# An LSTM-like recurrence: one of four state operations a step goes from VectorE to GpSimd

## The chip, the core and the metric

The kernel runs on one core of a Trainium2 chip, as one program. The metric is the device time of one execution in microseconds (us); the median of several runs counts. A core has five engines with a queue each: TensorE (PE in the profile; its weight loads are PEld), VectorE (DVE), ScalarE (ACT), GpSimd (POOL) and SyncE (SP). They work in parallel and wait for each other by semaphores.

## What is computed

The reference takes 3125 rows of 256 features and 50000 edges through four graph layers, each followed by a feed-forward part. The second of these parts is a recurrence over the 3125 rows, and it alone is touched by the change:

```python
def step(carry, xs):
    h, c = carry
    xi_t, xf_t, xg_t, xo_t = xs
    i_t = jax.nn.sigmoid(xi_t + h @ V_i)
    f_t = jax.nn.sigmoid(xf_t + h @ V_f)
    g_t = jnp.tanh(xg_t + h @ V_c)
    o_t = jax.nn.sigmoid(xo_t + h @ V_o)
    c_new = h * c + i_t * g_t
    h_new = o_t * jnp.tanh(c_new)
    return ((h_new, c_new), h_new)
(_, _), hs = lax.scan(step, (h0, c0), (xi, xf, xg, xo))
```

The new state c is h * c + i * g; the gate f has no effect on the output.

## The kernel before

The stages run one after the other, with a barrier of the engines between them. The recurrence is the stage of `Sweeps.run`. It doesn't go through the 3125 rows one by one: they are cut into 125 chains of 25 rows (`NC` and `L`), all chains take a step at once, and `FREE` = 9 sweeps over the 25 rows pass each chain's last state on to the next chain as its start. That makes 225 steps, written out one by one. At the end the largest change of the last sweep is computed (L2057 to L2070); with the inputs here it lets the kernel go on without further sweeps.

A state has 256 values. They lie as two halves (x = 0 and 1) of 128 partitions each, with the 125 chains along the columns. So h, c and each of the three gates used is 2 x 128 x 125 float32, and a step has six gate rows (`g` = 0 to 5): the candidate and the input gate of half 0, the same of half 1, and the output gate of halves 0 and 1. What each engine does in a step `n`, in the order of its queue:

- **TensorE** (L1970): for each `g` two products of a 128x128 weight block with half `y` of the old h. In float32 each product is two matmul instructions in the trace, so there are 24. First come the three products `g` = 0, 1, 2 with half 0 of h, then the same with half 1, and then the rest. The step begins when half 0 of the new h is there; half 1 is first needed by its seventh matmul instruction. `then_inc(gated, 1)` reports a finished `g`.
- **ScalarE**: sets the inputs of the output gates into PSUM (L2011), the gates `g` = 0 to 3 (L2001) into `Gt`, tanh of half 0 of c into `t3` (L2006, `state(n, 0)`), the output gates `g` = 4 and 5 (L2001), tanh of half 1 of c (`state(n, 1)`). Each raises `acted` by 1.
- **VectorE**: puts the inputs of coming gates into PSUM (L2024), `t1` = old h * old c for both halves (L2046); then for x = 0 and x = 1 `t2` = `Gt[x]` * `Gt[4 + x]` (L2028) and new c = `t1` + `t2` (L2030); then half 0 of the new h (L2034, `output(n, 0)`), inputs (L2024), half 1 of the new h (L2034), inputs. Each raises `stepped`, ten times in a step.
- **GpSimd** and SyncE have no instruction in these steps.

An engine runs its queue in the order written, so an instruction that waits holds all behind it. `t1`, `t2`, `t3`, `Gt` and `Cs` (c within a sweep) exist once and are reused in each step.

Of the kernel before, what the change touches and what calls it, by code (L numbers as in the profile page):

```python
# [16 lines left out]
ALU = mybir.AluOpType  # L17
# [1885 lines left out]
class Sweeps:  # L1903
# [33 lines left out]
    def run(self, sweeps, again):  # L1937


        k, nc = self.k, self.k.nc  # L1940
        gated, acted, stepped = k.loop
        XG, HS, V, Gt, t1, t2, t3, df, ft = (self.XG, self.HS, self.V, self.Gt, self.t1, self.t2, self.t3, self.df,
                                             self.ft)
        first, steps = 0, sweeps * L

        def sums(n, g, count=1):
            at = g + 6 * (n % 2) if g < 2 else g
            return k.PS[:, at:at + count, 0:NC]

        with k.block() as block:  # L1950
            @block.tensor
            def _(e):
                for b in range(8):
                    e.matmul(k.PS[:, b, 0:NC], V[:, 0, 0, :], k.ident[:, 0:NC], start=True, stop=True)

            if again:
                @block.vector
                def _(e):
                    e.tensor_copy(self.H[0][:, :, :], self.H[1][:, :, :])
                    e.tensor_copy(self.C[0][:, :, :], self.C[1][:, :, :])  # L1960
            else:
                @block.gpsimd
                def _(e):
                    for b in self.H + self.C:
                        e.memset(b[:, :, :], 0.0)
        with k.block() as block:
            @block.tensor
            def _(e):
                def product(n, g, y):
                    return e.matmul(sums(n, g)[:, 0, :], V[:, y, (4, 0, 5, 1, 2, 3)[g], :], self.old_h(n)[:, y, :],  # L1970
                                    start=False, stop=y == 1, skip_group_check=True)

                for n in range(first, first + steps):
                    r = n - first
                    e.wait_ge(stepped, 10 * r - 1 if r > 0 else 2)
                    product(n, 0, 0)
                    product(n, 1, 0)
                    if r > 0:
                        e.wait_ge(stepped, 10 * r)
                    product(n, 2, 0)  # L1980
                    if r > 0:
                        e.wait_ge(stepped, 10 * r + 1)
                    product(n, 0, 1).then_inc(gated, 1)
                    product(n, 1, 1).then_inc(gated, 1)
                    product(n, 2, 1).then_inc(gated, 1)
                    if r > 0:
                        e.wait_ge(stepped, 10 * r + 2)
                    product(n, 3, 0)
                    product(n, 3, 1).then_inc(gated, 1)
                    e.wait_ge(acted, 9 * r + 1)  # L1990
                    for g in (4, 5):
                        product(n, g, 0)
                        product(n, g, 1).then_inc(gated, 1)
                e.wait_ge(stepped, 10 * steps + 7)
                e.transpose(k.PS[0:1, 7, 0:128], df[:, 2:3], k.ident[:, :]).then_inc(gated, 1)

            @block.scalar
            def _(e):
                def gate(n, g, row):
                    e.wait_ge(gated, 6 * (n - first) + g + 1)  # L2000
                    e.activation(Gt[:, row, :], sums(n, g)[:, 0, :],  # L2001
                                 ACT.Tanh if row >= 4 else ACT.Sigmoid).then_inc(acted, 1)

                def state(n, x):
                    e.wait_ge(stepped, 10 * (n - first) + 6 + 2 * x)
                    e.activation(t3[:, x, :], self.new_c(n)[:, x, :], ACT.Tanh).then_inc(acted, 1)  # L2006

                for n in range(first, first + steps):
                    if n > first:
                        e.wait_ge(acted, 9 * (n - first) - 1)  # L2010
                    e.activation(sums(n, 4, 2), XG[:, n % L, 4:6, :], ACT.Copy).then_inc(acted, 1)  # L2011
                    gate(n, 0, 4)
                    gate(n, 1, 0)
                    gate(n, 2, 5)
                    gate(n, 3, 1)
                    state(n, 0)
                    gate(n, 4, 2)
                    gate(n, 5, 3)
                    state(n, 1)

            @block.vector
            def _(e):
                def inputs(n, g, row, count=1):
                    e.tensor_copy(sums(n, g, count), XG[:, n % L, row:row + count, :]).then_inc(stepped, 1)  # L2024

                def state(n, x):
                    e.wait_ge(acted, 9 * (n - first) + 3 + 2 * x)
                    e.tensor_tensor(t2[:, x, :], Gt[:, x, :], Gt[:, 4 + x, :], ALU.mult).then_inc(stepped, 1)  # L2028
                    e.wait_ge(stepped, 10 * (n - first) + 5 + 2 * x)
                    e.tensor_tensor(self.new_c(n)[:, x, :], t1[:, x, :], t2[:, x, :], ALU.add).then_inc(stepped, 1)  # L2030

                def output(n, x):
                    e.wait_ge(acted, 9 * (n - first) + 7 + 2 * x)
                    e.tensor_tensor(self.new_h(n)[:, x, :], Gt[:, 2 + x, :], t3[:, x, :],  # L2034
                                    ALU.mult).then_inc(stepped, 1)

                inputs(first, 0, 0, 2)
                inputs(first, 2, 2, 2)
                for n in range(first, first + steps):
                    r = n - first  # L2040
                    if r > 0:
                        e.wait_ge(acted, 9 * r - 6)
                    inputs(n + 1, 0, 0, 2)
                    if r > 0:
                        e.wait_ge(stepped, 10 * r + 1)
                    e.tensor_tensor(t1[:, :, :], self.old_h(n), self.old_c(n), ALU.mult).then_inc(stepped, 1)  # L2046
                    state(n, 0)
                    state(n, 1)
                    output(n, 0)
                    inputs(n + 1, 2, 2)  # L2050
                    output(n, 1)
                    inputs(n + 1, 3, 3)
                h = [b[:, :, 1:NC] for b in (self.H[(sweeps + 1) % 2], self.H[sweeps % 2])]
                c = [b[:, :, 1:NC] for b in (self.C[(sweeps + 1) % 2], self.C[sweeps % 2])]
                nb = NC - 1
                e.wait_ge(stepped, 10 * steps + 1)
                e.tensor_tensor(t1[:, :, 0:nb], h[1], h[0], ALU.subtract).then_inc(stepped, 1)  # L2057
                e.tensor_tensor(t2[:, :, 0:nb], c[1], c[0], ALU.subtract).then_inc(stepped, 1)
                e.tensor_copy(HS[:, L - 1, :, :], self.new_h(first + steps - 1))
                e.wait_ge(stepped, 10 * steps + 4)  # L2060
                e.tensor_reduce(df[:, 0:1], t1[:, :, 0:nb], AX.XY, ALU.max,
                                apply_absolute_value=True).then_inc(stepped, 1)
                e.tensor_reduce(df[:, 1:2], t2[:, :, 0:nb], AX.XY, ALU.max,
                                apply_absolute_value=True).then_inc(stepped, 1)
                e.wait_ge(stepped, 10 * steps + 6)
                e.tensor_tensor(df[:, 2:3], df[:, 0:1], df[:, 1:2], ALU.max).then_inc(stepped, 1)
                e.wait_ge(gated, 6 * steps + 1)
                e.tensor_reduce(ft[:, 0:1], k.PS[0:1, 7, 0:128], AX.X, ALU.max).then_inc(stepped, 1)
                e.wait_ge(stepped, 10 * steps + 8)
                e.tensor_scalar(self.go_on[:, :], ft[:, 0:1], TOL, None, ALU.is_gt)  # L2070
        nc.multi_engine_barrier(list(mybir.ALL_ENGINES), sems_to_clear=range(gated.num, stepped.num + 1))


def gate_inputs(k, XG, V):
# [981 lines left out]
def program(nc, a):  # L3056
    k = Core(nc, a)
    with ExitStack() as top:
# [6 lines left out]
        k.XR = nc.dram_tensor("rows_x", (N, D), f32).ap()  # L3065
        k.YT = nc.dram_tensor("rows_y", (2 * N + P + SLOTS * 128, D), f32).ap()
        k.EP = nc.dram_tensor("table", (ROWE, W * 4), f32).ap()
        k.loop = [nc.alloc_semaphore(s) for s in ("gated", "acted", "stepped")]
        k.slow = [nc.alloc_semaphore(s) for s in ("slow_step", "slow_landed0", "slow_landed1", "slow_landed2")]
        k.early = Sig(nc.alloc_semaphore("counts_early"))  # L3070
        k.first_out = [Sig(nc.alloc_semaphore(s)) for s in ("first_neg_out", "first_adj_out")]
# [95 lines left out]
```

## Time and profile before

| what | us |
|---|---|
| median of 3 runs (4396.59 to 4404.05) | 4402.93 |
| the profiled execution | 4404.55 |
| its span, first to last instruction | 4402.2 |
| the 225 steps of the recurrence, 2085 to 2821 | 736 |
| one step, from one start of TensorE to the next | 3.26 |

The profile is one execution. Its page gives busy times over the whole span, in which the stages have different limits; a question about the recurrence is answered by views that are cut to its stretch. Within it the steps repeat with almost equal times, so the rows of one step stand for all.

### The profile page before, as it was taken

To read this page: it belongs to the slowest core of one execution; us is meant where nothing else is said; L and a number is where in the kernel's file an instruction comes from. 1 tells how busy PE (TensorE), PEld (TensorE's weight loads), DVE (VectorE), ACT (ScalarE), POOL (GpSimd) and SP (SyncE) were. 2 spreads that over 40 slices of the span, in tenths; PEclk is the share of its full clock that TensorE was granted. 3 is DMA by queue.
4 is the path that set the end of the run, shared out by engine and by line. 5 is a ranking of instruction groups with operands and counts; after the bars stand their busy time and mean duration, and the time that the engine had idled before them with its cause. 6 is when DMAs were issued, how large, how long until landed. Compare 5 with 4: busy or idle time off the path is not lost. (4 is left out here: it accounts for less than half of the span.)

```text
span 4402.2 us, 67329 instructions
## 1 busy us (share of the span) xinstructions
PE 3539.8 (80%) x23858; PEld 3112.2 (71%) x23858; DVE 2759.3 (63%) x7024; ACT 1645.3 (37%) x4317; POOL 1261.6 (29%) x1266
## 2 busy tenths in 40 slices
PE   4677874755777876998999999799999699959696
PEld 3565653643565665784888888689999699949695
DVE  6899996563888848873888888732234433353444
ACT  1344442212444444562666666521110223320131
POOL 6777751635777710000000000000000122200263
PEclk8788786977887887999999999999998799979798
DMA  5455543244555563500000000143444311153424
GB/s 157 133 159 144 158 117 106 89 109 120 145 159 143 158 157 111 139 12 15 1 1 1 1 1 1 39 116 108 122 117 159 106 38 38 34 136 108 138 72 130
DMA packets 196536, 418.06 MB, mean 95 GB/s; under 512 B 54821, under 2 KB 127659, under 8 KB 195840
## 3 DMA queue, kind: packets, MB, share of 16 engines
q1 hardware_dynamic: 135296, 250.07, 19.8%
q0 software_dynamic: 60928, 164.04, 13.1%
q8 instruction: 171, 2.80, 0.3%
q14 instruction: 141, 1.16, 0.1%
HBM read 329.61 MB, written 84.35 MB: 94 GB/s over the span
## 5 line engine op out<-in xcount | busy, mean ns | idle before, releaser
L825 POOL DMA_INDIRECT sb<-features,sb x850 | 836.3, 984 | 262.1 <-issue 258.5
L1970 PE MATMUL ps<-sb 128*128 128x125 f32 x5400 | 662.1, 279 | 74.0 <-DVE sb L2034 72.9
L1970 PEld LDWEIGHTS ps<-sb 128*128 128x128 f32 x5400 | 619.8, 192 | 116.3 <-DVE sb L2034 115.0
L2269 PE MATMUL ps<-sb 125*125 125x256 f16 x5000 | 571.9, 275 | 15.8 <-DVE sb L2369 15.8
L2269 PEld LDWEIGHTS ps<-sb 125*125 125x125 f16 x5000 | 559.4, 138 | 21.0 <-issue 16.0
L136 POOL IOTA sb<- 128x56 f32 (+9 forms) x30 | 5.5, 219 | 1645.7 <-POOLq L105 1562.1
L2001 ACT ACTIVATE sb<-ps 128x125 f32<-128x125 f32 x1350 | 344.4, 273 | 232.5 <-PE ps L1970 202.7
L2982 ACT ACTIVATE sb<-ps,sb 128x128 f32<-128x128 f32 x784 | 221.1, 376 | 551.3 <-PE ps L2910 551.3
L1122 PE MATMUL ps<-sb 128*125 128x260 f32 x1700 | 385.7, 386 | 11.3 <-PEq L1120 10.8
L2910 PE MATMUL ps<-sb 128*128 128x128 f32 x3136 | 385.6, 279 | 1.9 <-DVE sb L2951 1.9
L1122 PEld LDWEIGHTS ps<-sb 128*125 128x125 f32 x1700 | 317.9, 189 | 93.6 <-issue 42.3
L2910 PEld LDWEIGHTS ps<-sb 128*128 128x128 f32 x3136 | 371.5, 195 | 2.6 <-DVE sb L2951 2.5
L2924 PE MATMUL ps<-sb 128*128 x1568 | 366.3, 380 | 0.0
L2924 PEld LDWEIGHTS ps<-sb 128*128 128x128 f32 x1568 | 285.6, 191 | 32.3 <-issue 0.3
L613 PE MATMUL ps<-sb 128*125 128x392 bf16 x850 | 247.2, 473 | 69.1 <-PEq L611 67.5
L2887 POOL DMA_INDIRECT rows_y<-sb x168 | 193.0, 1149 | 380.0 <-DVE sb L2963 365.0
L1343 PE MATMUL ps<-sb 125*125 125x257 f32 x1250 | 280.1, 386 | 17.2 <-DVE sb L1441 10.8
L1343 PEld LDWEIGHTS ps<-sb 125*125 125x125 f32 x1250 | 237.2, 191 | 58.2 <-issue 16.7
L613 PEld LDWEIGHTS ps<-sb 128*125 128x125 bf16 x850 | 166.4, 204 | 137.3 <-issue 76.1
L2944 DVE COPY sb<-sb 128x512 f32 (+2 forms) x168 | 133.9, 797 | 182.3 <-PE ps L2910 181.8
L983 DVE TENSOR_TENSOR sb<-sb,ps 128x1560 f32<-128x1560 f32 x150 | 244.3, 1684 | 1.7
L2963 DVE TENSOR_TENSOR sb<-ps,sb 128x256 f32<-128x256 f32 x168 | 71.3, 425 | 271.0 <-PE ps L2924 271.0
(323 smaller groups left out, 5272.9 us busy)
## 6 DMA issues: line engine op xcount, KB each, us to landing
sb<-adj SPq DMA_DIRECT2D x125, 683.6 KB
neg<-sb SPq DMA_DIRECT2D x25, 683.6 KB
adj<-sb SPq DMA_DIRECT2D x25, 683.6 KB
sb<-neg SPq DMA_DIRECT2D x25, 683.6 KB
sb<-rows_y SPq DMA_DIRECT2D x30, 560.0 KB
sb<-in_L_ffn_W SPq DMA_DIRECT2D x16, 1024.0 KB, 12.7
sb<-features,sb POOLq DMA_INDIRECT x850
sb<-adj SPq DMA_DIRECT2D x125, 79.3 KB
```

Of the source, the lines that this page charges most:

```text
L613: r = e.matmul(k.PS[0:P, 2 + x, 0:392], dt[:, w, :], self.hots[w % 4][:, 392 * x:392 * x + 392], start=w == 0, stop=w == W - 1)
L825: e.indirect_dma_start(hgs[i % 4][:, w, :], None, k.HR, indirect(ids[i % 3][:, w:w + 1])).then_inc(*hg_in[i % 4].by(16))
L983: e.tensor_tensor(v, v, shares[:, w0:w1, :].unsqueeze(3).broadcast_to([128, w1 - w0, 4, 65]), ALU.mult).then_inc(scaled_token.sem, 1)
L1122: m = e.matmul(k.PS[0:P, 6, 0:260], wides[u % 2][:, w, :], hgs[u % 4][:, w, 0:260], start=w == 0, stop=w == W - 1)
L1343: m = e.matmul(k.PS[0:P, n, 0:257], work[u % 7][:, n * P:n * P + P], HA[:, j, 0:257], start=j == 0, stop=j == T - 1)
L1970: return e.matmul(sums(n, g)[:, 0, :], V[:, y, (4, 0, 5, 1, 2, 3)[g], :], self.old_h(n)[:, y, :], start=False, stop=y == 1, skip_group_che ...
L2001: e.activation(Gt[:, row, :], sums(n, g)[:, 0, :], ACT.Tanh if row >= 4 else ACT.Sigmoid).then_inc(acted, 1)
L2269: m = e.matmul(self.k.PS[0:P, v % 2, 0:D], self.ads[v % self.RING][:, j * P:j * P + P], part[:, j, :], start=j == 0 and x == 0, stop=j == ...
L2887: e.indirect_dma_start(k.YT, indirect(keep.target[:, n:n + 1]), ys[n % 4][:, :], None).then_inc(*y_stored[n % 4].by(16))
L2910: m = e.matmul(hidden(n, c), w1s[n % deep][:, x, c, :], xts[n % 2][:, x, :], start=x == 0, stop=x == 1)
L2924: m = e.matmul(k.PS[:, 5 + n % 2, 0:D], hts[n % 2][:, c, :], w2f[:, bass.ds(v * (nh * D) + c * D, D)], start=c == 0, stop=c == nh - 1)
L2982: m = e.activation(hts[n % 2][:, c, :], hidden(n, c), ACT.Gelu, bias=cons[n % 4][:, c:c + 1])
```

## The change

The sum that gives half 1 of the new c is taken off VectorE's queue and given to GpSimd, which gets a loop over the steps for it. It has a semaphore of its own, `pooled`. GpSimd waits until `t2` of half 1 is done, adds, and raises `pooled`; ScalarE's tanh of half 1 waits for `pooled` in place of `stepped`. VectorE raises `stepped` nine times a step in place of ten, which changes the numbers in all other waits and nothing else about them. The core of the diff:

```diff
-        gated, acted, stepped = k.loop
+        gated, acted, stepped, pooled = k.loop
...
-                    e.wait_ge(stepped, 10 * r - 1 if r > 0 else 2)
+                    e.wait_ge(stepped, 9 * r - 1 if r > 0 else 2)
...
                 def state(n, x):
-                    e.wait_ge(stepped, 10 * (n - first) + 6 + 2 * x)
+                    if x == 0:
+                        e.wait_ge(stepped, 9 * (n - first) + 6)
+                    else:
+                        e.wait_ge(pooled, n - first + 1)
                     e.activation(t3[:, x, :], self.new_c(n)[:, x, :], ACT.Tanh).then_inc(acted, 1)
...
+            @block.gpsimd
+            def _(e):
+                for n in range(first, first + steps):
+                    e.wait_ge(stepped, 9 * (n - first) + 7)
+                    e.tensor_tensor(self.new_c(n)[:, 1, :], t1[:, 1, :], t2[:, 1, :], ALU.add).then_inc(pooled, 1)
...
                     e.tensor_tensor(t2[:, x, :], Gt[:, x, :], Gt[:, 4 + x, :], ALU.mult).then_inc(stepped, 1)
-                    e.wait_ge(stepped, 10 * (n - first) + 5 + 2 * x)
-                    e.tensor_tensor(self.new_c(n)[:, x, :], t1[:, x, :], t2[:, x, :], ALU.add).then_inc(stepped, 1)
+                    if x == 0:
+                        e.wait_ge(stepped, 9 * (n - first) + 5)
+                        e.tensor_tensor(self.new_c(n)[:, 0, :], t1[:, 0, :], t2[:, 0, :], ALU.add).then_inc(stepped, 1)
```

VectorE's queue in the second step, before. `sb311` holds the gate inputs, `sb312` all h of a sweep, `sb328` is c, `sb329` is `Gt`, `sb330` to `sb332` are `t1` to `t3`:

```order
L2024 COPY ps<-sb311 128x2x125 [waits acted]
L2046 TENSOR_TENSOR sb330<-sb312,sb328 128x250 [waits stepped]
L2028 TENSOR_TENSOR sb331<-sb329 128x125 [waits acted]
L2030 TENSOR_TENSOR sb328<-sb330,sb331 128x125 [waits stepped]
L2028 TENSOR_TENSOR sb331<-sb329 128x125 [waits acted]
L2030 TENSOR_TENSOR sb328<-sb330,sb331 128x125 [waits stepped]
L2034 TENSOR_TENSOR sb312<-sb329,sb332 128x125 [waits acted]
L2024 COPY ps<-sb311 128x125
L2034 TENSOR_TENSOR sb312<-sb329,sb332 128x125 [waits acted]
L2024 COPY ps<-sb311 128x125
```

The same step of VectorE now (all lines behind the new ones have moved down by 9 or 10, L2028 being L2037, L2034 being L2044):

```order
L2033 COPY ps<-sb311 128x2x125 [waits acted]
L2056 TENSOR_TENSOR sb330<-sb312,sb328 128x250 [waits stepped]
L2037 TENSOR_TENSOR sb331<-sb329 128x125 [waits acted]
L2040 TENSOR_TENSOR sb328<-sb330,sb331 128x125 [waits stepped]
L2037 TENSOR_TENSOR sb331<-sb329 128x125 [waits acted]
L2044 TENSOR_TENSOR sb312<-sb329,sb332 128x125 [waits acted]
L2033 COPY ps<-sb311 128x125
L2044 TENSOR_TENSOR sb312<-sb329,sb332 128x125 [waits acted]
L2033 COPY ps<-sb311 128x125
```

The second sum is gone, and half 0 of h follows the second product directly. GpSimd's queue around the loop, now; the memsets and the branches are there before too:

```order
L1965 MEMSET sb 128x252 x4
L105 UNCONDITIONAL_BRANCH
L48 UNCONDITIONAL_BRANCH [waits barrier_Pool_Activation_PE_DVE_SP_gather]
L2028 TENSOR_TENSOR sb<-sb 128x125 [waits stepped] x225
L105 UNCONDITIONAL_BRANCH
```

The row of L2028 is new: 225 sums, each with its wait.

## Rows read from the trace of the kernel before

**Rows 1.** The page's head and part 1: busy time, share of the span, instructions.
```profile
span 4402.2 us, 67329 instructions
...
PE 3539.8 (80%) x23858; PEld 3112.2 (71%) x23858; DVE 2759.3 (63%) x7024; ACT 1645.3 (37%) x4317; POOL 1261.6 (29%) x1266
```

**Rows 2.** Busy time by stretch: the 225 steps. The first row names the columns.
```profile
core 0: us, PE busy (x) PEld busy (x) DVE busy (x) ACT busy (x) POOL busy (x), PEclk, DMA share, GB/s
2085.00:2821.00 736.00, 662.07 (x5400) 619.77 (x5400) 605.24 (x2250) 500.15 (x2027) 0.00 (x0) 1.00 0.01 1
```

**Rows 3.** View of line L2034, the new h: who waited for it (us, times).
```profile
  PE ps L1970: 72.9, 224
```

**Rows 4.** Instructions in order of time, 2400 to 2407 us.
```profile
start us, us, engine line op out<-in xcount [idle before <-releaser]
...
2402.12 0.29 DVE L2030 TENSOR_TENSOR sb<-sb 128x125 f32<-128x125 f32 x1
2402.15 0.28 ACT L2001 ACTIVATE sb<-ps 128x125 f32<-128x125 f32 x1 [0.17 <-PE ps L1970]
2402.44 0.31 ACT L2006 ACTIVATE sb<-sb 128x125 f32<-128x125 f32 x1
2402.46 0.29 DVE L2028 TENSOR_TENSOR sb<-sb 128x125 f32<-128x125 f32 x1
2402.66 0.66 ACT L2001 ACTIVATE sb<-ps 128x125 f32<-128x125 f32 x2
2402.79 0.29 DVE L2030 TENSOR_TENSOR sb<-sb 128x125 f32<-128x125 f32 x1
2402.99 0.28 DVE L2034 TENSOR_TENSOR sb<-sb 128x125 f32<-128x125 f32 x1
...
2403.22 0.30 ACT L2006 ACTIVATE sb<-sb 128x125 f32<-128x125 f32 x1
...
2403.33 2.94 PE L1970 MATMUL ps<-sb 128*128 128x125 f32 x24 [0.32 <-DVE sb L2034]
...
2403.55 0.29 DVE L2034 TENSOR_TENSOR sb<-sb 128x125 f32<-128x125 f32 x1
...
2405.06 0.29 DVE L2028 TENSOR_TENSOR sb<-sb 128x125 f32<-128x125 f32 x1 [0.38 <-ACT sb L2001]
2405.38 0.29 DVE L2030 TENSOR_TENSOR sb<-sb 128x125 f32<-128x125 f32 x1
...
2406.59 0.60 PE L1970 MATMUL ps<-sb 128*128 128x125 f32 x3 [0.32 <-DVE sb L2034]
```

**Rows 5.** The same view of ScalarE, 2402.67 to 2402.70: one output gate alone.
```profile
2402.66 0.26 ACT L2001 ACTIVATE sb<-ps 128x125 f32<-128x125 f32 x1
```

**Rows 6.** In order of time, VectorE and GpSimd where GpSimd waits for VectorE.
```profile
718.79 0.41 DVE L170 TENSOR_SCALAR sb<-sb 125x256 f32<-125x256 f32 x1
...
719.28 13.71 POOL L3023 TENSOR_TENSOR sb<-sb 125x6400 f32<-125x6400 f32 x1 [16.51 <-DVE sb L170]
```

**Rows 7.** In order of time, VectorE while GpSimd runs its other large tensor_tensor.
```profile
55.16 13.76 POOL L1829 TENSOR_TENSOR sb<-sb 125x6400 f32<-125x6400 f32 x1
...
63.09 0.62 DVE L447 TENSOR_SCALAR_CACHE_REDUCE sb<-sb 125x400 bf16<-125x400 int32 x1
...
63.76 5.21 DVE L450 SCALAR_TENSOR_TENSOR sb<-sb 125x25 f32<-125x25 f32 x1
```

**Rows 8.** Groups of GpSimd by shape: busy us, mean ns of one, idle before.
```profile
L2704 POOL TENSOR_SCALAR_AFFINE_SELECT sb<-sb 125x125 f32<-125x125 f32 x3 | 0.9, 297 | 0.2
...
L2702 POOL MEMSET sb<- 125x125 f32 x3 | 0.6, 200 | 0.0
...
L303 POOL MEMSET sb<- 128x1 f32 x1 | 0.1, 89 | 0.0
```

**Rows 9.** In order of time, TensorE from its seventh matmul of the step.
```profile
2404.10 0.39 PE L1970 MATMUL ps<-sb 128*128 128x125 f32 x2
```

**Rows 10.** In order of time, VectorE with no GpSimd tensor_tensor beside it.
```profile
74.20 0.19 DVE L473 SCALAR_TENSOR_TENSOR sb<-sb 125x25 f32<-125x25 f32 x1
```

More of the change, by code:

```diff
@@ L1978, in _ @@
                     if r > 0:
-                        e.wait_ge(stepped, 10 * r)
+                        e.wait_ge(stepped, 9 * r)
                     product(n, 2, 0)
                     if r > 0:
-                        e.wait_ge(stepped, 10 * r + 1)
+                        e.wait_ge(stepped, 9 * r + 1)
                     product(n, 0, 1).then_inc(gated, 1)
@@ L1986, in _ @@
                     if r > 0:
-                        e.wait_ge(stepped, 10 * r + 2)
+                        e.wait_ge(stepped, 9 * r + 2)
                     product(n, 3, 0)
@@ L1993, in _ @@
                         product(n, g, 1).then_inc(gated, 1)
-                e.wait_ge(stepped, 10 * steps + 7)
+                e.wait_ge(stepped, 9 * steps + 7)
                 e.transpose(k.PS[0:1, 7, 0:128], df[:, 2:3], k.ident[:, :]).then_inc(gated, 1)
@@ L2044, in _ @@
                     if r > 0:
-                        e.wait_ge(stepped, 10 * r + 1)
+                        e.wait_ge(stepped, 9 * r + 1)
                     e.tensor_tensor(t1[:, :, :], self.old_h(n), self.old_c(n), ALU.mult).then_inc(stepped, 1)
@@ L2055, in _ @@
                 nb = NC - 1
-                e.wait_ge(stepped, 10 * steps + 1)
+                e.wait_ge(stepped, 9 * steps + 1)
                 e.tensor_tensor(t1[:, :, 0:nb], h[1], h[0], ALU.subtract).then_inc(stepped, 1)
@@ L2059, in _ @@
                 e.tensor_copy(HS[:, L - 1, :, :], self.new_h(first + steps - 1))
-                e.wait_ge(stepped, 10 * steps + 4)
+                e.wait_ge(stepped, 9 * steps + 4)
                 e.tensor_reduce(df[:, 0:1], t1[:, :, 0:nb], AX.XY, ALU.max,
@@ L2064, in _ @@
                                 apply_absolute_value=True).then_inc(stepped, 1)
-                e.wait_ge(stepped, 10 * steps + 6)
+                e.wait_ge(stepped, 9 * steps + 6)
                 e.tensor_tensor(df[:, 2:3], df[:, 0:1], df[:, 1:2], ALU.max).then_inc(stepped, 1)
@@ L2068, in _ @@
                 e.tensor_reduce(ft[:, 0:1], k.PS[0:1, 7, 0:128], AX.X, ALU.max).then_inc(stepped, 1)
-                e.wait_ge(stepped, 10 * steps + 8)
+                e.wait_ge(stepped, 9 * steps + 8)
                 e.tensor_scalar(self.go_on[:, :], ft[:, 0:1], TOL, None, ALU.is_gt)
-        nc.multi_engine_barrier(list(mybir.ALL_ENGINES), sems_to_clear=range(gated.num, stepped.num + 1))
+        nc.multi_engine_barrier(list(mybir.ALL_ENGINES), sems_to_clear=range(gated.num, pooled.num + 1))
 def gate_inputs(k, XG, V):
@@ L3067, in program @@
         k.EP = nc.dram_tensor("table", (ROWE, W * 4), f32).ap()
-        k.loop = [nc.alloc_semaphore(s) for s in ("gated", "acted", "stepped")]
+        k.loop = [nc.alloc_semaphore(s) for s in ("gated", "acted", "stepped", "pooled")]
         k.slow = [nc.alloc_semaphore(s) for s in ("slow_step", "slow_landed0", "slow_landed1", "slow_landed2")]
```

## The prediction

> **What bounds the kernel now.** I read the page's head first, then the busy times of the recurrence's stretch, then who waits for whom there, and last the instructions of single steps in order of time.
>
> The page says only that GpSimd is busy 29% of the span [rows 1]. The view of the stretch says more: from 2085 to 2821 us GpSimd runs nothing, TensorE is busy 662 of 736 us at a granted clock of 1.00 (the 2.4 GHz level), and VectorE 605 us [rows 2]. 736 us over 225 steps is 3.27 us a step. The view of the line that makes the new h (L2034) shows that TensorE, matmul side, waited 224 times for it, 72.9 us in all, 0.33 us each [rows 3]. So a step is the 2.94 us of its 24 matmuls and a 0.32 us gap which ends when VectorE has made the first half of h. TensorE is no full bound: what moves that instruction moves the step.
>
> Now one step by its rows [rows 4]. TensorE starts a step at 2403.33, the next at 2406.59: 3.26 us. The gates of a half come through ScalarE; the product `Gt[0]*Gt[4]` starts at 2405.06, the sum c0 at 2405.38 (c0 of the step before: 2402.12, done 2402.41), tanh of c0 at 2402.44, then the output gate of the first half at 2402.66. That gate alone takes 0.26 us [rows 5], so it is done at 2402.92. A gate that ends reaches VectorE 0.03 us later (gate at 2402.15 + 0.28 = 2402.43, the product L2028 starts at 2402.46). The first half's h (L2034) could therefore start at 2402.95. It starts at 2402.99, because the sum c1 (L2030, 2402.79), the instruction that the change moves, stands before it and VectorE takes the next one 0.20 us after a start. From its end, 2403.27, TensorE needs 0.06 us: 2403.33.
>
> **What is removed.** 225 sums of 0.29 us on VectorE, 65 us of busy time. Only what they hold back counts: 2402.99 - 2402.95 = 0.04 us a step. Over 224 gaps that is 9 us (rounding of the rows to 0.01 us allows 0.05 us, 11 us). The rest lies beside the ScalarE chain and is hidden anyway.
>
> **What is added.** 225 sums on GpSimd, a wait for the product before them, and a wait of ScalarE for them. I place it in the step [rows 4]: the second product ends at 2402.46 + 0.29 = 2402.75. From VectorE's end to a GpSimd tensor_tensor the trace has one row: 718.79 + 0.41 = 719.20 to 719.28, 0.08 us [rows 6]. So the sum starts at 2402.83. Its length D isn't in the trace. The two large ones take 13.76 and 13.71 us for 6400 elements a partition [rows 6, 7], 2.15 ns an element, 0.27 us for 125. The lower bound adds the shortest fixed cost that a row shows, 0.09 us of a memset of one column [rows 8]: 0.36 us. The upper bound starts from the one-input instruction of 125 columns that reads SBUF, 0.30 us [rows 8], and adds the second stream, 0.27 less the 0.11 us by which 125 columns of memset (0.20) exceed one: 0.46 us. I take 0.40, between them, as a read adds something to a memset's fixed part. The Trainium skill ("GPSIMD Engine Reference", Elementwise — side-by-side cycle accounting) gives 4497 ns for 2048 elements; less 2048 x 2.15 this leaves 0.09 us fixed, and the sum would by it be the lower one below, 4416. So c1 is done at 2402.83 + 0.40 = 2403.23.
>
> **Is the added chain itself late?** Tanh of c1 starts at 2403.22 today, behind ScalarE's last gate; with VectorE's handoff to ScalarE (2402.41 to 2402.44, 0.03) it would start at 2403.26 or a little later. Second half of h: 0.33 us behind that (2403.22 to 2403.55), so 2403.59, done 2403.88, at TensorE 2403.94. The first matmul that needs it, the seventh of the step, starts at 2404.10 [rows 9]. So this costs nothing: 0.16 us of cover is left. With D at 0.46 it is 0.10.
>
> **What it collides with.** The other instruction that wants to run in 2402.83 to 2403.23 is the first half of h on VectorE, a tensor_tensor that reads two SBUF tiles. The trace shows what such an instruction does beside a GpSimd tensor_tensor: while L1829 ran, 55.16 to 68.92, the one-input instructions of L447 kept their 0.62 us, but the first one with two SBUF inputs, L450, of only 125x25, stood from 63.76 to 68.97, 5.21 us, and ended 0.05 us after GpSimd did [rows 7]. The same instruction and shape at L473 takes 0.19 us [rows 10]. So VectorE's second operand waited until GpSimd was nearly done. The Trainium skill ("SBUF — State Buffer", Who interferes with whom) speaks against this change in the same way: such a pair shares a read interface, the one that issues first has it for its whole instruction, and the other fully blocks. Of the blocking the trace agrees; to the letter, with nothing of the second instruction done before the first has ended, it gives 4457, where the row gives the sum below.
>
> **The sum.** GpSimd comes first here, at 2402.83 against 2402.95. L450 ended 0.05 us behind GpSimd with an own length of 0.19; the half of h has 0.28, so it ends 0.05 + 0.09 = 0.14 us behind: 2403.23 + 0.14 = 2403.37, and TensorE starts at 2403.43 in place of 2403.33. The gain of 0.04 is swallowed in this, and the step is 0.10 us longer: 224 x 0.10 = 22.4 us. With D = 0.36 it is 0.06, 13 us; with D = 0.46, 0.16, 36 us. The profiled execution took 4404.55 us for a span of 4402.2, and the median of the three runs is 4402.93; outside the recurrence nothing changes, so the sum goes on the median: 4402.93 + 22.4 = **4425.3**, own range 4416 to 4439. What is late next: the loop now runs TensorE, gate at 2402.15, second product, GpSimd's sum, half of h; the c0 chain has 0.14 us of air.
>
> **Rivals.**
> 1. *No collision, so faster.* If so short a sum gets out of the way, or only long ones hold the pair, h starts at 2402.95 and 9 to 11 us go: 4393. For it: the moved instruction really is what holds h back, and c1 has 0.16 us of cover. Against: the row of L450. It decides at D below about 0.26 us (2402.83 + 0.26 + 0.14 + 0.06 = 2403.29), or if GpSimd doesn't hold the operand at all. The line to faster by 0.2%, 8.8 us, falls inside it.
> 2. *VectorE comes first.* If GpSimd needs over 0.12 us more than the 0.08 of that one row, h runs at 2402.95 and the sum waits for it, until 2403.15 (0.20 behind its start) or 2403.23 (its end). Then c1 is done at 2403.55 to 2403.63, tanh at 2403.58 to 2403.66, the second half of h at 2403.91 to 2403.99, at TensorE 2404.26 to 2404.34. The seventh matmul, 0.77 us behind a start [rows 9], would be due at 2403.29 + 0.77 = 2404.06: late by 0.20 to 0.28, less the 0.04 gained, 36 to 54 us: 4439 to 4457.
> 3. *Full exclusion.* If h starts its whole length only after GpSimd's recorded end, it ends at 2403.23 + 0.28 = 2403.51, TensorE starts at 2403.57, 0.24 late, 54 us: 4457. For it: GpSimd's instructions here are short, so their tail may weigh more. Against: L450 ended only 0.05 us behind GpSimd, though its own length is 0.19.
> 4. *A short hold.* The recorded length of the sum has a tail in which the operands are free; if it is longer than in L1829's case, h is delayed by under 0.04 us: 4400 to 4411, no measurable change.
>
> **Chances.** Forecast 0.58; rival 1 0.14; rival 2 0.13; rival 3 0.09; rival 4 0.06. Above 0.2% counts as told from no change. Slower: 0.58 + 0.13 + 0.09 = 0.80, and all of these lie over 8.8 us. Of rival 1 I give half, 0.07, to faster, as its 9 to 11 us lie at the line; same is the other half and rival 4, 0.13. Range: 4412 (the lower bound with the rows' rounding) to 4460 takes in the forecast and rivals 2 and 3, 0.80.
>
> **What would show it.** On VectorE the line of h (L2044 then) has two kinds in place of one 0.28 us: the first half near 0.40 us, from some 0.12 us after GpSimd's start to 0.14 after its end; the second stays 0.29. TensorE's idle before a step grows from 0.32 to 0.42, put down to that same line or to GpSimd; matmuls stay at 2.94 us a step and the clock at full. GpSimd has 225 sums of 0.36 to 0.46 us. Rival 1: h at 0.28 us and a gap of 0.28. Rival 2: h at 0.28, a long sum or a late one, and a second gap in front of the seventh matmul. Rival 3: h over 0.5 us. I am wrong above all if a VectorE instruction this short isn't held, for which I have one row, or if the sum is far off 0.40 us.

## The result, and the profile after

| what | before | after |
|---|---|---|
| median, 6 runs each | 4402.24 us (4396.59 to 4414.25) | 4436.30 us (4429.71 to 4438.63) |
| ratio of after to before | | 1.0073 (1.0058 to 1.0088) |
| span of the profiled execution | 4402.2 us | 4433.4 us |
| one step of the recurrence | 3.26 us | 3.41 us |
| TensorE's wait for half 0 of h, 224 times | 72.9 us | 106.4 us |

The change makes the kernel slower by 0.73%. The forecast was 4425.3 with a range of 4412 to 4460.

The head of the page after, as [rows 1]. GpSimd has 225 instructions and some 98 us more, VectorE 225 instructions less and only 4 us less busy time (2759.3 before), although 65 us of sums have left it (some 45 us of busy time: each sum's last 0.09 us lay under the next instruction, 2402.79 + 0.29 against 2402.99):

```profile
span 4433.4 us, 67329 instructions
...
PE 3544.4 (80%) x23858; PEld 3115.8 (70%) x23858; DVE 2755.2 (62%) x6799; ACT 1665.8 (38%) x4317; POOL 1359.7 (31%) x1491
```

Busy time by stretch for the 225 steps after, with the columns of [rows 2]. TensorE has the same 662.07 us in 5400 matmuls and the same clock; only the time between them has grown:

```profile
2083.00:2852.00 769.00, 662.07 (x5400) 619.77 (x5400) 602.30 (x2023) 521.46 (x2025) 100.84 (x225) 1.00 0.00 1
```

The view of the line that makes h, L2044 after, which answers to [rows 3]; duration in ns as min/median/max. First its row before, then after. It took 280 to 292 ns; now one of the two in a step takes up to 483:

```profile
L2034 DVE TENSOR_TENSOR sb<-sb x450: 280/287/292, 2089.8 to 2821.1; 128x125 f32<-128x125 f32 x150
```

```profile
L2044 DVE TENSOR_TENSOR sb<-sb x450: 287/318/483, 2087.6 to 2852.4; 128x125 f32<-128x125 f32 x150
...
  PE ps L1970: 106.4, 224
```

And the same view of GpSimd's sum, L2028, which didn't exist before:

```profile
L2028 POOL TENSOR_TENSOR sb<-sb x225: 447/448/450, 2087.3 to 2851.6; 128x125 f32<-128x125 f32 x113
```

One step in order of time, answering to [rows 4]:

```profile
2400.55 0.28 ACT L2001 ACTIVATE sb<-ps 128x125 f32<-128x125 f32 x1 [0.17 <-PE ps L1970]
2400.84 0.31 ACT L2009 ACTIVATE sb<-sb 128x125 f32<-128x125 f32 x1
2400.86 0.29 DVE L2037 TENSOR_TENSOR sb<-sb 128x125 f32<-128x125 f32 x1
2401.05 0.67 ACT L2001 ACTIVATE sb<-ps 128x125 f32<-128x125 f32 x2
2401.22 0.45 POOL L2028 TENSOR_TENSOR sb<-sb 128x125 f32<-128x125 f32 x1 [2.96 <-DVE sb L2037]
2401.34 0.48 DVE L2044 TENSOR_TENSOR sb<-sb 128x125 f32<-128x125 f32 x1 [0.19 <-ACT sb L2001]
2401.71 0.31 ACT L2009 ACTIVATE sb<-sb 128x125 f32<-128x125 f32 x1
...
2401.88 2.94 PE L1970 MATMUL ps<-sb 128*128 128x125 f32 x24 [0.47 <-DVE sb L2044]
...
2405.29 1.94 PE L1970 MATMUL ps<-sb 128*128 128x125 f32 x15 [0.47 <-DVE sb L2044]
```

Read it against the step before. The second product (L2037) ends at 2401.15. GpSimd starts at 2401.22 (78 to 80 ns later in all steps) and is done at 2401.67. The instruction for half 0 of h is released at 2401.34, earlier in the step than before, just as its freed place in the queue promised: 0.48 us behind the product's start where it was 0.53. But it then takes 0.48 us and ends at 2401.82, 0.15 behind GpSimd. TensorE follows 0.06 later. A step is 2405.29 - 2401.88 = 3.41 us, 0.15 more, and 224 x 0.15 = 34 us, the measured difference.

A note on reading: the blocked instruction doesn't show a gap in front of it, it shows as a long instruction. VectorE's busy time hides a wait here.

### The profile page after: what moved, and what is told of

It reads as the page before. It is cut to its first block and busy times, and to the rows that moved or that the text cites. A ratio compares the mean times of both kernels' runs of the same rounds, so it can differ in the third digit from the quotient of the medians.

```text
span 4433.4 us, 67329 instructions
## 1 busy us (share of the span) xinstructions
PE 3544.4 (80%) x23858; PEld 3115.8 (70%) x23858; DVE 2755.2 (62%) x6799; ACT 1665.8 (38%) x4317; POOL 1359.7 (31%) x1491
## 5 line engine op out<-in xcount | busy, mean ns | idle before, releaser
L1970 PE MATMUL ps<-sb 128*128 128x125 f32 x5400 | 662.1, 279 | 107.5 <-DVE sb L2044 106.4
L2028 POOL TENSOR_TENSOR sb<-sb 128x125 f32<-128x125 f32 x225 | 100.9, 448 | 669.9 <-DVE sb L2037 669.9
```

## The experiments

The theory: while GpSimd reads SBUF for its sum, VectorE's second SBUF operand isn't served. The main rival: the step is delayed by the sum of half 1 being late, through its length and handoffs. In what follows the step is the distance of two starts of TensorE in the trace. Rows are rounded to 0.01 us; the medians over all 224 distances of a run are within 0.01 of the step given here. The first four experiments in the table ran on a chip on which the kernel before takes 4968.42 us, and split_sum_sbuf on one where it takes 4984.14. The 24 matmuls take 2.94 us there too (psum_tanh_alone), but the steps begin at 2643 to 2670 us in place of 2078 to 2085, so the additional time lies ahead of them. Ratios are always to the kernel before on the same chip; where this run or the kernel before ran once, the ratio is only a rough check, and the trace carries the reading.

| run | half 0 of h, us | GpSimd, us | step, us | time to that of before |
|---|---|---|---|---|
| before | 0.28 | none | 3.26 | 1 |
| after | 0.48 | 0.45 | 3.41 | 1.0073 (1.0058 to 1.0088) |
| psum_tanh | 0.29 | 0.45 | 3.26 | 1.0006 (0.9997 to 1.0015) |
| psum_tanh_alone | 0.28 | none | 3.26 | 0.9989 (0.9980 to 0.9998) |
| late_sum | 0.29 | 0.49 | 3.52 | 1.0124 (1.0109 to 1.0140) |
| sum_behind_h | 0.29 | none | 3.42 | 1.0069 (1.0053 to 1.0084) |
| idle_sum | 0.54 | 0.45 | 3.66 | 1.021, one run of each |
| half_idle_sum | 0.41 | 0.32 | 3.54 | 1.013, one run |
| idle_copy | 0.37 | 0.29 | 3.49 | 1.013, one run of each |
| idle_memset | 0.29 | 0.20 | 3.42 | 1.009, one run of each |
| split_sum | 0.28 | 0.32 | 3.23 | 0.9979 (0.9970 to 0.9988) |
| split_sum_sbuf | 0.34 | 0.32 | 3.29 | 1.0013 (1.0004 to 1.0023) |

### One operand moved out of SBUF: psum_tanh and psum_tanh_alone

The edit, made in the changed kernel (psum_tanh) and in the kernel before (psum_tanh_alone):

```diff
+        def tanh(x):
+            return k.PS[:, 2, 128:128 + NC] if x == 0 else t3[:, 1, :]
...
-                    e.activation(t3[:, x, :], self.new_c(n)[:, x, :], ACT.Tanh).then_inc(acted, 1)
+                    e.activation(tanh(x), self.new_c(n)[:, x, :], ACT.Tanh).then_inc(acted, 1)
...
-                    e.tensor_tensor(self.new_h(n)[:, x, :], Gt[:, 2 + x, :], t3[:, x, :],
+                    e.tensor_tensor(self.new_h(n)[:, x, :], Gt[:, 2 + x, :], tanh(x),
```

> The changed kernel, but tanh of half 0 is written to PSUM (bank 2, columns 128 to 252), so that the instruction that makes half 0 of h reads one SBUF tile and one PSUM tile. Theory (GpSimd's sum holds VectorE's second SBUF operand): the hold is gone, that instruction takes 0.28 us again in place of 0.48 and starts 0.03 us after the output gate; the step is 3.21 to 3.22 us (3.26 less the 0.047 by which the sum used to hold it back), 224 x 0.047 = 10 us under the kernel before, about 4392. Rival (the length of GpSimd's sum or its handoffs delay the step through c1): the step stays 3.41 us, about 4436.

> The kernel before, with only tanh of half 0 moved to PSUM. Both theories: nothing, 4402 within 0.2%, step 3.26 us, since VectorE's sum of half 1 still stands before the instruction; if reading PSUM is by itself faster or slower, this run shows it.

In order of time in psum_tanh (L2040 is the product, L2031 GpSimd's sum, L2047 makes h, L2012 is tanh):

```profile
3002.28 0.45 POOL L2031 TENSOR_TENSOR sb<-sb 128x125 f32<-128x125 f32 x1 [2.81 <-DVE sb L2040]
3002.39 0.29 DVE L2047 TENSOR_TENSOR sb<-sb,ps 128x125 f32<-128x125 f32 x1 [0.19 <-ACT sb L2004]
...
3002.74 2.99 PE L1973 MATMUL ps<-sb 128*128 128x125 f32 x24 [0.28 <-DVE sb L2047]
3002.76 0.31 ACT L2012 ACTIVATE sb<-sb 128x125 f32<-128x125 f32 x1
...
3003.11 0.29 DVE L2047 TENSOR_TENSOR sb<-sb 128x125 f32<-128x125 f32 x1 [0.23 <-ACT sb L2012]
...
3006.00 1.19 PE L1973 MATMUL ps<-sb 128*128 128x125 f32 x8 [0.28 <-DVE sb L2047]
```

GpSimd's sum still takes 0.45 us and still runs first, but half 0 of h, which now reads one SBUF tile and one PSUM tile, takes 0.29 beside it. The hold on the second SBUF operand is shown, and the rival falls as the cause of the 34 us: with the late sum of half 1 still there, the step is back at 3.26. psum_tanh_alone has the same step without GpSimd, so PSUM by itself gives nothing to it. (Its 0.1% less is not to be found in its steps and stays open.)

The expected gain of 10 us is a miss, though. TensorE's gap fell to 0.28 as foreseen, but the 24 matmuls took 2.98 to 2.99 us in place of 2.94. Something within the train was late by 0.04: the seventh matmul keeps its start at 0.77 us but lasts some 0.31 us in place of 0.28. Behind it is the weight load that goes before the seventh matmul. First that load in the kernel before, in the step that starts at 2403.33, then in psum_tanh in the step that starts at 3002.74:

```profile
2403.99 0.19 PEld L1970 LDWEIGHTS ps<-sb 128*128 128x128 f32 x1
```

```profile
3003.45 0.19 PEld L1973 LDWEIGHTS ps<-sb 128*128 128x128 f32 x1
```

0.66 us into the step before, 0.71 now, and 3003.45 is 0.05 behind the end of half 1 of h (3003.11 + 0.29). So the wait for half 1 is met by the weight load, which runs 0.11 us ahead of the matmul at 0.77. The sum on GpSimd makes half 1 late for that.

### VectorE first: late_sum

```diff
                     e.wait_ge(stepped, 9 * (n - first) + 7)
+                    e.wait_ge(acted, 9 * (n - first) + 7)
```

> The changed kernel, with GpSimd waiting also for the output gate of half 0 (acted at 9n+7), so that VectorE's half 0 of h starts first (0.03 us after the gate, GpSimd some 0.08). Hold theory, with the rule that who comes second waits: h keeps 0.28 us, the sum of 0.45 starts or works only from about 0.20 us behind the start of h, c1 is done at 3.53 us of the step, the second half of h is 0.27 late for the seventh matmul; step 3.48 us, about 4451. If GpSimd isn't held by VectorE: c1 at 3.37, 0.11 late, step 3.32 us, about 4416.

```profile
3000.08 0.29 DVE L2045 TENSOR_TENSOR sb<-sb 128x125 f32<-128x125 f32 x1 [0.19 <-ACT sb L2001]
3000.19 0.49 POOL L2029 TENSOR_TENSOR sb<-sb 128x125 f32<-128x125 f32 x1 [3.04 <-ACT sb L2001]
...
3000.43 3.25 PE L1970 MATMUL ps<-sb 128*128 128x125 f32 x24 [0.28 <-DVE sb L2045]
...
3003.95 0.82 PE L1970 MATMUL ps<-sb 128*128 128x125 f32 x5 [0.28 <-DVE sb L2045]
```

With the order reversed VectorE keeps its 0.29 us, and it is GpSimd that grows, from 0.45 to 0.49. Who starts first isn't held. GpSimd loses only 0.04 us, though the two overlap for 0.18 (3000.19 to 3000.37); the last section comes back to this. The step is 3.52 us; expected was 3.48. The sum was done 0.05 sooner than reckoned, and the weight load wanted half 1 0.10 sooner. This is the second rival of the prediction, and its place in the list is confirmed: slower than what happened.

### A base without GpSimd: sum_behind_h

```diff
                     e.tensor_tensor(t2[:, x, :], Gt[:, x, :], Gt[:, 4 + x, :], ALU.mult).then_inc(stepped, 1)
+                    if x == 0:
+                        total(n, x)
+
+                def total(n, x):
                     e.wait_ge(stepped, 10 * (n - first) + 5 + 2 * x)
...
                     output(n, 0)
+                    total(n, 1)
                     inputs(n + 1, 2, 2)
```

> The kernel before with VectorE's own sum of half 1 put behind half 0 of h; GpSimd idle. Half 0 of h starts at 2.88 us of the step, the sum at 3.08, tanh at 3.41, half 1 of h at 3.74, at TensorE 4.08, where the seventh matmul would be due at 3.215 + 0.769 = 3.98: step 3.31 to 3.32 us, 12 us more than before, about 4414. Both theories expect this; it is the base for runs in which GpSimd does work that nobody waits for.

The step is 3.42 us and not 3.31. The start of a step, then VectorE's second half of h, then the loads of TensorE beside it:

```profile
3003.04 3.13 PE L1970 MATMUL ps<-sb 128*128 128x125 f32 x24 [0.28 <-DVE sb L2038]
```

```profile
3003.56 0.29 DVE L2038 TENSOR_TENSOR sb<-sb 128x125 f32<-128x125 f32 x1 [0.17 <-ACT sb L2006]
```

```profile
3003.90 0.30 PEld L1970 LDWEIGHTS ps<-sb 128*128 128x128 f32 x2
```

Again the weight load starts 0.05 behind half 1 of h, 0.86 into a step that began at 3003.04, and not the matmul: the missing 0.10 us. Also worth noting: on VectorE the place in front of half 0 of h was the better one for this sum.

### Work of GpSimd that nobody waits for

These kernels are sum_behind_h plus a GpSimd instruction on scratch tiles at the moment of the changed kernel's sum. They leave out nothing of the computation.

```diff
+                for n in range(first, first + steps):
+                    if n > first:
+                        e.wait_ge(pooled, n - first)
+                    e.wait_ge(stepped, 10 * (n - first) + 7)
+                    e.tensor_tensor(self.S[0][:, :], self.S[1][:, :], self.S[2][:, :], ALU.add).then_inc(pooled, 1)
```

In idle_memset the last line is a memset, in idle_copy a tensor_copy, in half_idle_sum it takes columns 0 to 61.

> As sum_behind_h (all work on VectorE), but GpSimd adds two constant scratch tiles of 128x125 into a third at the moment at which the changed kernel has its sum; nobody waits for it. Hold theory: half 0 of h takes 0.48 us in place of 0.28 and the step is 0.20 us longer than in sum_behind_h, about 3.51 us. Rival (the delay comes through the data or the handoffs of c1): the step is that of sum_behind_h, 3.31 us.

> As idle_sum, with a memset of the scratch tile (128x125, it writes SBUF and reads nothing). If only reads of GpSimd hold the operand: step as in sum_behind_h, 3.31 us, h 0.28 us. If any GpSimd instruction holds it: memset ends at 2.76 + 0.20 = 2.96, h is 0.08 behind its usual end at least where it ends 0.147 behind GpSimd's, no more than 3.16, so nothing either; then a hold would show only as a longer h.

> As idle_sum, with a copy of a scratch tile (one SBUF input). If one read stream holds the operand too: the copy takes about 0.30 us, ends at 3.06, h ends 0.147 behind it at 3.21 in place of 3.16, step 3.36 us. If only GpSimd's two-input instructions do: 3.31 us, h 0.28 us.

> As idle_sum, but GpSimd adds 62 of the 125 columns. Theory (the hold lasts as long as GpSimd's instruction and h ends 0.14 us behind it): 63 columns x 2.15 ns = 0.135 us less, GpSimd 0.31 us, h 0.41 in place of 0.54, step 3.66 - 0.135 = 3.53 us. Rival (a fixed price of sharing, whatever the length): the step stays 3.66 us.

In order of time, GpSimd's instruction, half 0 of h and TensorE's start, in idle_sum:

```profile
2402.59 0.29 DVE L2039 TENSOR_TENSOR sb<-sb 128x125 f32<-128x125 f32 x1
```

```profile
2403.03 0.45 POOL L2030 TENSOR_TENSOR sb<-sb 128x125 f32<-128x125 f32 x1 [3.22 <-DVE sb L2039]
2403.08 0.54 DVE L2049 TENSOR_TENSOR sb<-sb 128x125 f32<-128x125 f32 x1 [0.19 <-ACT sb L2004]
...
2403.67 3.13 PE L1973 MATMUL ps<-sb 128*128 128x125 f32 x24 [0.53 <-DVE sb L2049]
```

half_idle_sum:

```profile
2400.12 0.32 POOL L2030 TENSOR_TENSOR sb<-sb 128x62 f32<-128x62 f32 x1 [3.22 <-DVE sb L2039]
2400.17 0.41 DVE L2049 TENSOR_TENSOR sb<-sb 128x125 f32<-128x125 f32 x1 [0.20 <-ACT sb L2004]
```

idle_copy:

```profile
2402.32 0.29 POOL L2030 COPY sb<-sb 128x125 f32<-128x125 f32 x1 [3.20 <-DVE sb L2039]
2402.38 0.37 DVE L2049 TENSOR_TENSOR sb<-sb 128x125 f32<-128x125 f32 x1 [0.19 <-ACT sb L2004]
```

idle_memset:

```profile
2403.41 0.20 POOL L2030 MEMSET sb<- 128x125 f32 x1 [3.21 <-DVE sb L2039]
2403.49 0.29 DVE L2049 TENSOR_TENSOR sb<-sb 128x125 f32<-128x125 f32 x1 [0.20 <-ACT sb L2004]
```

The step that follows in idle_sum starts at 2407.34:

```profile
2407.34 0.93 PE L1973 MATMUL ps<-sb 128*128 128x125 f32 x6 [0.54 <-DVE sb L2049]
```

Nobody waits for GpSimd in these, and yet its sum costs VectorE 0.25 us and the step 0.24 (3.66 against 3.42, which sum_behind_h has on one chip and idle_memset on that of idle_sum). That settles the question without any data path through GpSimd. Half the columns take 0.13 us off GpSimd's instruction, 0.13 off VectorE's and 0.12 to 0.13 off the step: the price grows with the length of GpSimd's instruction and isn't a fixed one; the expectation of 3.53 was met. A copy, with one input, holds VectorE too: h ends at 2402.75, 0.14 behind the copy. A memset, which reads nothing, runs across the start of h for 0.12 us and leaves it at 0.29; the step is that of the base. This doesn't show that a memset holds nothing: without any hold h ends 0.16 us behind the memset, and the held ones end 0.14 behind GpSimd, so a memset that held VectorE as the sum does would leave the same trace. A longer memset would tell; none ran beside such an instruction. In idle_sum h ends at 2403.62, 0.14 behind GpSimd; the price is 0.25 and not the 0.20 expected because GpSimd started late, at 2403.03, 0.14 to 0.15 behind the product's end at 2402.88.

### A version that is faster than both: split_sum and split_sum_sbuf

VectorE keeps most of the sum, GpSimd takes the last 30 columns beside it, and the tanh of half 0 lies in PSUM as above (in split_sum_sbuf it doesn't). Core of the edit to the kernel before, `CUT` = 95:

```diff
+                for n in range(first, first + steps):
+                    e.wait_ge(stepped, 10 * (n - first) + 7)
+                    e.tensor_tensor(self.new_c(n)[:, 1, CUT:NC], t1[:, 1, CUT:NC], t2[:, 1, CUT:NC],
+                                    ALU.add).then_inc(pooled, 1)
...
+                    if x == 1:
+                        e.wait_ge(pooled, n - first + 1)
...
-                    e.tensor_tensor(self.new_c(n)[:, x, :], t1[:, x, :], t2[:, x, :], ALU.add).then_inc(stepped, 1)
+                    w = NC if x == 0 else CUT
+                    e.tensor_tensor(self.new_c(n)[:, x, 0:w], t1[:, x, 0:w], t2[:, x, 0:w], ALU.add).then_inc(stepped, 1)
```

> Tanh of half 0 in PSUM as in psum_tanh_alone, VectorE sums columns 0 to 94 of half 1 and GpSimd 95 to 124 at the same time; ScalarE waits for both. No hold on h, since it reads one SBUF tile. VectorE's shorter sum lets h start 30 / 0.96 = 31 ns earlier; GpSimd's takes 0.448 - 95 x 2.15 ns = 0.24 us and is itself held behind VectorE's for up to 0.1, done at 3.05 to 3.11 of the step, early enough for tanh at 3.15 to 3.20. Expected: step 3.23 us, 224 x 0.03 = 7 us under the kernel before (0.9985). Rival (cover of half 1 used up, as in psum_tanh, where the weight load of the seventh matmul came 0.04 late): step 3.26 us, no change.

> split_sum with tanh of half 0 back in SBUF, so that half 0 of h reads two SBUF tiles. Hold theory: GpSimd's sum of 30 columns still ends at 3.084 of the step (2.763 + 0.321), h starts at 2.89 and ends 0.14 behind GpSimd, at 3.23 in place of 3.17; step 3.28 us, 0.02 above the kernel before (4407, no measurable change) and 0.055 above split_sum. Rival (the gain of split_sum is only the shorter sum on VectorE, and PSUM plays no part): step 3.23 us, 4395.

split_sum in order of time:

```profile
2400.19 0.26 DVE L2044 TENSOR_TENSOR sb<-sb 128x95 f32<-128x95 f32 x1
2400.24 0.32 POOL L2031 TENSOR_TENSOR sb<-sb 128x30 f32<-128x30 f32 x1 [2.90 <-DVE sb L2041]
2400.37 0.28 DVE L2048 TENSOR_TENSOR sb<-sb,ps 128x125 f32<-128x125 f32 x1
...
2400.70 2.94 PE L1974 MATMUL ps<-sb 128*128 128x125 f32 x24 [0.28 <-DVE sb L2048]
...
2403.93 0.38 PE L1974 MATMUL ps<-sb 128*128 128x125 f32 x1 [0.28 <-DVE sb L2048]
```

split_sum_sbuf:

```profile
3001.68 0.26 DVE L2041 TENSOR_TENSOR sb<-sb 128x95 f32<-128x95 f32 x1
3001.72 0.32 POOL L2028 TENSOR_TENSOR sb<-sb 128x30 f32<-128x30 f32 x1 [2.96 <-DVE sb L2038]
3001.85 0.34 DVE L2045 TENSOR_TENSOR sb<-sb 128x125 f32<-128x125 f32 x1
...
3002.24 1.94 PE L1971 MATMUL ps<-sb 128*128 128x125 f32 x15 [0.34 <-DVE sb L2045]
```

In split_sum half 0 of h starts 0.18 behind the sum's start in place of 0.20, TensorE's gap is 0.28 and the train is 2.94 again: 3.23 us a step, 4394.04 us, 0.21% under the kernel before (9 us, of which the steps explain 8). GpSimd's 30 columns take 0.32 us, not 0.24; VectorE's sum starts first and most likely holds it, which fits late_sum but wasn't varied alone. Without PSUM, h is held again, to 0.34 us and 0.15 behind GpSimd's end, and the gain turns into 0.13% of loss. Both halves of the recipe are needed: PSUM alone has a step of 3.26 us (psum_tanh_alone), the split sum alone 3.29, both together 3.23.

## Why the prediction was right

**What bounds the step.** Right. TensorE's wait for half 0 of h moved the step one to one in every run in which the train was undisturbed.

**The gain of 0.04 us from the freed queue place.** Right: the instruction was released 0.05 us sooner (after), and where nothing held it (psum_tanh), the gap fell from 0.32 to 0.28.

**The placement of GpSimd's sum.** The handoff, foreseen with 0.08 from one row, was 0.08 (78 to 80 ns). The order, GpSimd first, was as foreseen.

**Its length D.** The one term of the sum that was mis-sized: 0.40 taken, 0.45 measured (448 ns), inside the stated 0.36 to 0.46 and near its upper end. half_idle_sum shows why. 62 columns take 316 ns, 125 take 448: 2.1 ns a column, as the large sums had it, and 0.19 us fixed. The fixed part was about that of the one-input instruction of [rows 8] (0.30 - 0.11 = 0.19), and not between it and the memset's 0.09. By the sum of the prediction, D = 0.45 gives 2403.28 + 0.14 + 0.06 = 2403.48, 0.15 us a step, 4402.93 + 34 = 4437: the measured time to 1 us. The estimate by the Trainium skill ("GPSIMD Engine Reference", Elementwise — side-by-side cycle accounting), 0.09 us fixed and 4416, was further off.

**The collision.** Right in kind and in size. The single row of L450 [rows 7] told both that a VectorE instruction with two SBUF inputs is held and when it comes free: 0.14 us behind GpSimd's end was expected, 0.15 measured (143 to 148 ns in all steps). It was carried from an instruction of 0.19 us to one of 0.28 on one row's strength, a row that repeats in all twelve traces (L450 ends 0.05 to 0.06 us behind L1829); the runs bear it out for that one length of VectorE and for GpSimd's of 0.29 to 0.45 us. Of the rule in the Trainium skill ("SBUF — State Buffer", Who interferes with whom), these runs agree with two parts: two SBUF inputs are held against a GpSimd instruction that reads (idle_sum, idle_copy), and the first one isn't held (late_sum). That one that only writes doesn't hold them is its third part, and no run here shows it: idle_memset fits, but would look the same with a hold. Taken to the letter, with the whole length of the second behind the recorded end of the first, it is too hard by 0.13 us here: h would have ended 0.28 behind GpSimd. That was rival 3, and it fell. In late_sum it is too hard by as much on the other side, 0.04 us of loss for 0.18 of overlap.

**The cover of half 1.** Wrong by 0.11 us, without effect on the forecast, since a longer step gives cover back. The prediction took the seventh matmul, at 2404.10 [rows 9], as what waits for half 1; it is that matmul's weight load, at 2403.99. So the cover before was 0.10 us (2403.55 + 0.29 + 0.05 = 2403.89), and the change uses it up: without a collision it would have been late by 0.04 us, which is all of the 0.04 gained.

**The rivals.** Rival 1, no collision, was priced at 4393. psum_tanh is that case on the chip, and it makes no difference (1.0006): its price was wrong by the term above. So with a sum of 0.45 us this change had nothing to win even without a collision. Rival 2 was measured as late_sum: 1.24% slower, where 0.8 to 1.2% were reckoned. Rivals 3 and 4 fell.

## What to carry to other kernels

Before moving an elementwise instruction to GpSimd, look at what VectorE does in the same moments: if one of its instructions has two SBUF inputs and stands on the path, and GpSimd's, started first, reads SBUF, it ends some 0.14 us behind GpSimd's at the earliest, and shows as a long instruction rather than as a gap. One operand in PSUM took it out of the collision here (psum_tanh). And when you count the cover of an operand of a matmul, count to the weight load that carries the wait, not to the matmul.

## What the runs showed of the hardware that was not expected

- A copy on GpSimd (one input, 0.29 us) holds a two-input VectorE instruction as its two-input sum does: it ends 0.14 us behind the copy's end.
- In either order, the one that starts second loses the time for which the two records overlap, less 0.14 to 0.15 us. VectorE second, overlap and loss in us: 0.33 and 0.19 (after), 0.40 and 0.25 (idle_sum), 0.27 and 0.12 (half_idle_sum), 0.23 and 0.08 (idle_copy), 0.19 and 0.04 (split_sum_sbuf). GpSimd second: 0.18 and 0.04 (late_sum). This is read off the runs; none was made to test it.
- A GpSimd sum behind one semaphore wait started 0.08 us after its releaser's end (after); behind two waits, the first long met, 0.14 us (idle_sum, and late_sum: gate of 0.26 from 2999.79, start 3000.19). The copy and the memset behind two waits started after 0.13 and 0.12 us. That the second wait is the cause is inferred; no run varied it alone.
- A float32 tensor_tensor on GpSimd costs 0.19 us plus 2.1 ns a column, by 62 and 125 columns with two inputs in SBUF.
